# Exps over three PSUM banks and odd score tiles in the attention part of a ViT tower on one Trainium2 core

## The reference

```python
h = tok_embed(x)                                   # 16 x 1024 x 64
# attention on layernorm(h), 8 heads of 8 dimensions
scores = einsum('bihd,bjhd->bhij', q, k) / sqrt(8) + col_bias[None, :, None, :]
attn = softmax(scores, axis=-1)
h = h + einsum('bhij,bjhd->bihd', attn, v).reshape(B, N, D) @ Wo + bo
# experts on layernorm(h): 8 experts of 64 hidden units, the best 2 of a softmax router
h = h + tokens + sum_e combine[:, e] * (gelu(tokens @ w1[e] + b1[e]) @ w2[e] + b2[e])
```

## Time and profile before

| | us |
|---|---|
| median of three runs | 1386.28 |
| the profiled execution | 1381.28 |
| its span, first to last instruction | 1379.5 |
| TensorE matmuls busy | 1237.4 (90%) |
| VectorE busy | 833.8 (60%) |
| ScalarE busy | 1050.4 (76%) |
| mean granted TensorE clock | 0.985 of full speed |

### The profile page before, as it was taken

How to read it: one execution, slowest core, us unless ns; L and a number is a source line. 1 busy time by engine, 2 the same in 40 slices (tenths; PEclk the granted TensorE clock), 3 DMA queues, 4 the chain that set the end, 5 groups by cost and what they waited for, 6 DMA issues and landing times. The chain is left out here.

```text
span 1379.5 us, 29786 instructions
## 1 busy us (share of the span) xinstructions
PE 1237.4 (90%) x9442; PEld 368.5 (27%) x9443; DVE 833.8 (60%) x2165; ACT 1050.4 (76%) x1173; POOL 116.6 (8%) x113
## 2 busy tenths in 40 slices
PE   2179999998989898999999999999999988999998
PEld 1021222322222222222222222222222222333332
DVE  8734566575756575756565757565666256655555
ACT  0069998988889898989999999898989963333333
POOL 4300000000001000000000000000000000000000
PEclk9999999999999999999999999999999988999999
DMA  1222132322222222212131313131223011222221
GB/s 43 55 52 72 41 79 66 70 56 62 66 57 70 45 71 45 71 45 71 45 82 34 82 34 82 34 82 42 76 50 73 10 57 39 57 73 62 62 74 42
DMA packets 63101, 80.31 MB, mean 58 GB/s; under 512 B 26960, under 2 KB 27984, under 8 KB 63000
## 3 DMA queue, kind: packets, MB, share of 16 engines
q1 hardware_dynamic: 60828, 78.76, 22.7%
q10 hardware_dynamic: 1916, 0.55, 0.2%
q0 software_dynamic: 256, 0.01, 0.0%
HBM read 41.90 MB, written 37.27 MB: 57 GB/s over the span
## 5 line engine op out<-in xcount | busy, mean ns | idle before, releaser
L1025 ACT ACTIVATE probs<-psum 128x1024 f32<-128x1024 f32 x1024 | 956.6, 1080 | 91.1 <-PE psum L1154 86.9
L1170 PE MATMUL psum<-probs,VA 128*32 128x512 f32 x4096 | 553.5, 612 | 21.7 <-ACT probs L1025 16.1
L1154 PE MATMUL psum<-QA,KA 54*128 54x512 bf16 x2048 | 351.4, 389 | 36.7 <-ACTq L1044 9.0
L1154 PEld LDWEIGHTS psum<-QA,KA 54*128 54x128 bf16 x2048 | 81.6, 93 | 541.1 <-ACT probs L1025 511.1
L1308 ACT ACTIVATE act_h<-psum,b 128x512 f32<-128x512 f32 x128 | 87.8, 687 | 143.8 <-PE psum L1411 137.7
L1359 DVE TENSOR_TENSOR gated<-act_h,psum 128x512 f32<-128x512 f32 x128 | 87.8, 687 | 90.3 <-ACT act_h L1308 90.1
L1071 DVE STREAM_TRANSPOSE oT<-psum 128x512 f32<-128x512 f32 x64 | 45.9, 717 | 154.0 <-issue 85.5
L1170 PEld LDWEIGHTS psum<-probs,VA 128*32 128x32 f32 x4096 | 83.9, 108 | 150.0 <-issue 91.4
L1411 PE MATMUL psum<-m_x,w_parts 128*128 128x512 bf16 x384 | 108.3, 392 | 1.1 <-DMA m_cT<-cT_d 1.1
L1383 PE MATMUL psum<-gated,w 128*64 128x512 f32 x256 | 69.9, 624 | 0.0
L1025 ACT ACT_TABLE_LOAD x1 | 1.3, 1283 | 76.2 <-issue 76.2
(11 more groups left out here) (187 smaller groups left out, 1015.6 us busy)
## 6 DMA issues: line engine op xcount, KB each, us to landing
QA<-q_parts_d SPq DMA_DIRECT2D x64, 192.0 KB
KA<-k_parts_d SPq DMA_DIRECT2D x64, 192.0 KB
q_parts_d<-qk_parts SPq DMA_DIRECT2D x32, 192.0 KB, 2.5
k_parts_d<-qk_parts SPq DMA_DIRECT2D x32, 192.0 KB, 2.7
xT<-in_xT SPq DMA_DIRECT2D x16, 256.0 KB, 3.5
q_parts_d<-qk_parts SPq DMA_DIRECT2D x32, 128.0 KB, 2.6
k_parts_d<-qk_parts SPq DMA_DIRECT2D x32, 128.0 KB, 2.6
x_d<-x_stacks SPq DMA_DIRECT2D x16, 256.0 KB, 2.1
```

Of the source, the lines that this page charges most:

```text
L1025: nc.scalar.activation(probs[:, k % PROB_BUFS, :], score_buf(buf_of(k)), ACT.Exp).then_inc(exped, 1)
L1154: last = pe.matmul(score_buf(buf_of(k))[:, (g % 2) * BANK:(g % 2 + 1) * BANK], KA[rows_of(h, SCORE_ROWS), h // 2, jt * P:(jt + 1) * P], QA ...
L1170: last = pe.matmul(o_acc[32 * g:32 * g + 32, :], VA[:, jt, h, :], probs[:, k % PROB_BUFS, (g % 2) * BANK:(g % 2 + 1) * BANK], start=(jt == ...
```

## The change

A score *tile* is now three banks, or two for the last tile of each group of 32 scores: 10 x 3 + 2 = 32, so 11 tiles a group and 44 exps an image. PSUM holds two score buffers of three banks, `probs` four buffers of three banks. A tile no longer coincides with half a quad: `TILE_OF` gives the tile of each score, and on TensorE the small steps of a slot and the values of a quad are issued in the turn of the tile that completes the quad (values two tiles later). The thresholds of semaphores follow. The fallback keeps buffers of two banks.

```diff
-SCORE_BUFS = 3
-PROB_BUFS = 8
+WIDE = 3
+GROUP_TILES = [WIDE] * 10 + [2]
+TILES = GROUPS * len(GROUP_TILES)
+FIRST = ...  # first score of each tile
+TILE_OF = [t_ for t_ in range(TILES) for _ in range(FIRST[t_], FIRST[t_ + 1])]
+SCORE_BUFS = 2
+PROB_BUFS = 4
...
-                    nc.scalar.activation(probs[:, k % PROB_BUFS, :], score_buf(buf_of(k)),
+                    n = FIRST[t + 1] - FIRST[t]
+                    nc.scalar.activation(probs[:, t % PROB_BUFS, 0:n * BANK], score_buf(t)[:, 0:n * BANK],
                                          ACT.Exp).then_inc(exped, 1)
...
-                def scores(b, q):
-                    for g in range(4):
-                        k = 2 * q + g // 2
-                        if g % 2 == 0:
-                            if last_use(k) >= 0 or later(b):
-                                pe.wait_ge(exped, BLOCKS * b + last_use(k) + 1)
-                        h, ih, jt = head_of(q, g)
-                        last = pe.matmul(score_buf(buf_of(k))[:, (g % 2) * BANK:(g % 2 + 1) * BANK],
+                def scores(b, t):
+                    if t >= SCORE_BUFS or later(b):
+                        pe.wait_ge(exped, TILES * b + t - SCORE_BUFS + 1)
+                    for n, i in enumerate(range(FIRST[t], FIRST[t + 1])):
+                        h, ih, jt = head_of(i // 4, i % 4)
+                        last = pe.matmul(score_buf(t)[:, n * BANK:(n + 1) * BANK],
                                          KA[rows_of(h, SCORE_ROWS), h // 2, jt * P:(jt + 1) * P],
                                          QA[rows_of(h, SCORE_ROWS), h // 2, ih * BANK:(ih + 1) * BANK],
                                          start=True, stop=True)
-                        if g % 2:
-                            last.then_inc(scored, 1)
+                    last.then_inc(scored, 1)
...
-                    for q in range(QUADS):
-                        ...
-                        scores(b, q)
-                        for step in steps_of(q, not last, not first):
-                            ...
-                        if q >= LAG:
-                            values(b, q - LAG)
-                        elif not first:
-                            values(b - 1, QUADS + q - LAG)
+                    for t in range(TILES):
+                        ...
+                        scores(b, t)
+                        for slot in range(QUADS):
+                            if TILE_OF[4 * slot + 3] != t:
+                                continue
+                            for step in steps_of(slot, not last, not first):
+                                ...
+                        for q in range(QUADS):
+                            if TILE_OF[4 * q + 3] == t - LAG:
+                                values(b, q)
+                            elif TILE_OF[4 * q + 3] == t - LAG + TILES and not first:
+                                values(b - 1, q)
```

More of the change, by code:

```diff
@@ L40 @@
 QUADS = 2 * 2 * NCH
-BLOCKS = 2 * QUADS
 GROUPS = 4
+QUARTER = QUADS // GROUPS
+WIDE = 3
+GROUP_TILES = [WIDE] * 10 + [2]
+TILES = GROUPS * len(GROUP_TILES)
+FIRST = [0]
+for g_ in range(GROUPS):
+    for n_ in GROUP_TILES:
+        FIRST.append(FIRST[-1] + n_)
+TILE_OF = [t_ for t_ in range(TILES) for _ in range(FIRST[t_], FIRST[t_ + 1])]
 LAG = 2
-SCORE_BUFS = 3
-PROB_BUFS = 8
+SCORE_BUFS = 2
+PROB_BUFS = 4
 EVAC_SLOTS = {8 * g + 7 + LAG: g for g in range(3)}
@@ L52 @@
 POST = ["out_proj", "post_t0", "post_t1", "router", "combine_t"]
-ROUTER_EXP_BLOCK = 52
-BUF_TURN = 38
+ROUTER_EXP_TILE = 36
 PAIRS = NX // 2
@@ L198, in attention, with score_buf, fb_buf @@
         oT_norm = sb("oT_norm", [P, 2, BANK // 32, 32], F32)
[L200 to L209, removed]
+        def score_buf(t):
+            return psum[:, WIDE * BANK * (t % SCORE_BUFS):WIDE * BANK * (t % SCORE_BUFS + 1)]
+        def fb_buf(u):
+            return psum[:, 2 * BANK * (u % 2):2 * BANK * (u % 2 + 1)]
         o_acc = psum[:, 6 * BANK:7 * BANK]
@@ L1048, in body @@
                     flag = act.value_load(flags[0:1, ds(b, 1)], min_val=0, max_val=1)
[L1049 to L1053, removed]
+                    for t in range(TILES):
+                        if t % (TILES // 2) == 0:
+                            fallback(b, t // (TILES // 2), flag)
+                        exp_tile(b, t)
+                        if t == ROUTER_EXP_TILE and not first:
                             router_exp(aux_base(b) + aux_order(not last, True).index("router") + 1)
@@ L1184, in fallback @@
                             for n in range(2):
-                                last = pe.matmul(score_buf(u % 2)[:, n * BANK:(n + 1) * BANK],
+                                last = pe.matmul(fb_buf(u)[:, n * BANK:(n + 1) * BANK],
                                                  QA[rows_of(h, SHIFT_ROW), h // 2, c * P:(c + 1) * P],
@@ L1201, in body @@
                     order = aux_order(not last, not first)
[L1202 to L1213 removed]
+                    for t in range(TILES):
+                        if t % (TILES // 2) == 0:
+                            hg = t // (TILES // 2)
+                            pe.wait_ge(aug_loaded[hg], 16 * AUG_DMAS * (b + 1))
+                            fallback(b, hg, flag)
+                        scores(b, t)
[3 more added lines that the diff above has]
+                            for step in steps_of(slot, not last, not first):
+                                i = order.index(step)
+                                aux_step(step, b + 1 if step in PREP else b - 1, aux_base(b) + i + 1, aux_base(b) + i)
+                        for q in range(QUADS):
[3 more added lines that the diff above has]
+                                values(b - 1, q)
                 all_batches(pe, body)
[L1216 to L1217 removed]
+                for q in range(QUADS):
+                    if TILE_OF[4 * q + 3] >= TILES - LAG:
+                        values(NB - 1, q)
         inner.close()
```

27 lines of the change are left out of this document (14 added, 13 removed).

## The result

Four runs of the changed kernel took 1443.47 to 1457.21 us, the median 1451.34 us, against 1386.3: slower, ratio 1.0475 (95% interval 1.0409 to 1.0540). Forecast were 1435 us and 1403 to 1462. The profiled execution took 1443.5 us (62.2 us more than before's), so it is the fastest of the four, and the others had a lower mean clock (0.979 to 0.981 against 0.984). Two executions of the kernel before are left out of the comparisons: one of 2225.99 us beside the changed kernel's four, and one of 1436.38 us at a mean clock of 0.849 beside e5, e7, e8 and e9.

What follows compares the result with a forecast made beforehand. The prediction took ScalarE and TensorE as nearly equal bounds. TensorE's 62.3 us plus 5.5, 0.1 and 2.3 of waiting, less 0.9 and 0.3, gave 69.0 an image: 1435 us in all, range 1403 to 1462.

Steps and rivals of the forecast that it cites:

- Two bounds almost on top of each other: In a middle image of the kernel before, ScalarE needs 58.2 us plus stalls and TensorE 62.3, of 65.8.
- Wider exps, -1.0 us: On ScalarE, fewer and wider exps take 57.2 us an image in place of 58.2.
- Odd tiles, +5.5 us of TensorE: A tile of three scores costs what four did, 0.535 us, adding 5.5 us an image on TensorE.
- Rival C: Between small steps ScalarE keeps the pace and its saving of 1.0 to 1.2 us an image arrives: 1369 us, chance 0.07.
- Rival A: Left-over scores pair with the next tile's first at three places a group: no change, 1386 us, chance 0.06.
- Mutual waiting, 12 x 0.2: With two score buffers, TensorE waits 0.2 us for an exp three times a group: 2.3 us an image.
- Rival D: The two-buffer hand-over is worse, say 0.1 us of stall at every tile: +4.8 us an image, 1463 us, chance 0.11.
- Small steps: Steps between scores and values show nearly whole on ScalarE: one stall of about 1.3 us behind the projections, 0.8 at the transposes.
- VectorE: TensorE's waits for VectorE: 0.9 us before the post transposes and 0.3 before a group's first values go; image start +0.1.
- Sum: A middle image takes 69.0 us: 66.7 of TensorE and 2.3 of mutual waiting, +3.2 us.
- The clock: Stretches of lower TensorE clock behind the embedding add about 0.3 us an image, the same as before the change.
- Rival B: A TensorE with less idle time loses the low-clock stretches, and half the mutual waiting is absent: 1413 us, chance 0.14.

Runs made afterwards that it cites:

- e5: The kernel before with values three quads behind their scores in place of two (LAG = 3): 1621.5 us, ratio 1.172.
- e7: The changed kernel without the fallback's branches on VectorE, TensorE and ScalarE: 1408.9 us, ratio 1.018 to the kernel before.
- e8: The kernel before without the fallback's branches on VectorE, TensorE and ScalarE: 1352.8 us, ratio 0.977.
- e9: The changed kernel with six more, useless score matmuls ahead of each image's first values, where TensorE idles: 1442.8 us, ratio 1.044 to the kernel before.
- e3: The changed kernel with exps of at most two banks from the second image on, a third of their columns left out: 1436.0 us, ratio 1.038.
- e12: The changed kernel without the fallback's branches, third score matmul of each tile narrowed to 64 columns from the second image on: 1351.8 us, ratio 0.978.
- e11: The changed kernel without the fallback's branches, each three-score tile given a fourth matmul repeating its second score: 1413.8 us, ratio 1.022 to the kernel before.
- e1: The kernel before with two score buffers of two banks in place of three: 1443.2 us, ratio 1.043.
- e13: The kernel before with the scores of quad 3 issued directly behind the embedding, ahead of the first values: 1378.4 us, ratio 0.996.
- e4: The changed kernel with score tiles of four and two banks by turns, so every tile has whole pairs: 1602.6 us, ratio 1.159 to the kernel before.
- e10: The kernel before with LAG = 3 and VectorE's evacuations of slots 2 and 18 moved ahead of those slots' small steps: 1456.0 us, ratio 1.052.

## Why the prediction was right, point by point

- *Two bounds almost on top of each other.* Right. e3 shows that ScalarE no longer bounds; in e8 58 us of the 63.74 of an image are exps, which shows how little it was away from bounding before.
- *Wider exps, -1.0 us.* Right in the duration (1.34 from start to start). Of the 1.0 us, 0.3 an image is what e12 has over e8.
- *Odd tiles, +5.5 us of TensorE.* Right: 0.53 for three, as for four. e11 and e12 show it. Rival C (a tile of three at the time of two) fell. Rival A's pairing happens (0.75 for six at 736.87), but in one place an image and not in twelve, and the tile after the pair then waits 0.41 us for its exp (739.09); the time did not follow A. The prediction had expected it in two to four places, yet counted none in its sum.
- *Mutual waiting, 12 x 0.2.* Right: exps 1, 2, 5, 6, 12, 16, 23, 24, 27, 34, 38 and 39 of an image (counted from 0) start 0.14 to 0.19 late, with and without branches, 2.1 us in all. They are not three in every group, as forecast, but four, two, three and three. With the small steps' stalls there are 21 places, 11.1 us, in a full-clock image (709 to 778 us); forecast were 19 and 11.5. Rival D, a stall at every tile and 70.6 us an image, fell. e1 shows that the number of buffers matters by itself (+3.3 us), and e12 that two buffers of three banks are enough as soon as TensorE has room. So the cost is the two together; how much each has of it no run separates.
- *Small steps.* The stall of 1.3 behind the projections is there (1.22 of idle at 733.72), 0.75 at the transposes.
- *VectorE.* The 0.9 in front of the post transposes went. The 0.3 for an evacuation did not go: it is 0.66 (765.92) and gives ScalarE a stall of 0.8. At the turn of the loop TensorE waits 0.89, not 0.46; before, the values of one more quad had lain in it. The wait at the image's start was forecast at 1.4 to 1.5. It comes in two sizes, with the time that VectorE stands in "issue" ahead of its evacuation: 0.6 to 0.7 us in five of the middle images (5.8 to 5.9 us of issue) and 1.3 to 1.5 in eight (6.5 to 6.7, as in most images before). Why VectorE takes one or the other stays open.
- *Sum.* 69.0 us for a middle image; 68.6 to 68.7 at full clock, and 69.3 in the ninth, where the wait at the image's start is as long as forecast.
- *The clock: the term that was mis-sized.* I took 0.3 us an image, as before. Seven of the fifteen images have a low stretch and take 70.4 to 72.1 us, 2.2 more than the others. Not all of the 2.2 is the clock: in these images VectorE is late as well. Its evacuation in a full-clock image and in one with a low stretch, then TensorE in the latter:

```profile
714.25 0.72 DVE L1074 STREAM_TRANSPOSE oT<-psum 128x512 f32<-128x512 f32 x1 [5.93 <-issue]
360.86 0.72 DVE L1074 STREAM_TRANSPOSE oT<-psum 128x512 f32<-128x512 f32 x1 [6.55 <-issue]
```

```profile
358.38 1.95 PE L554 MATMUL psum<-w_tok,xT 64*128 64x64 f32 x16
361.68 1.93 PE L1171 MATMUL psum<-probs,VA 128*32 128x512 f32 x8 [1.35 <-ACT probs L1028]
363.54 1.03 PE L1155 MATMUL psum<-QA,KA 54*128 54x512 bf16 x3
364.50 1.32 PE L1171 MATMUL psum<-probs,VA 128*32 128x512 f32 x8
365.76 0.60 PE L1155 MATMUL psum<-QA,KA 54*128 54x512 bf16 x3
```

  The profile puts TensorE's wait of 1.35 us down to an exp; the evacuation ends at 361.58, 0.1 us before the values start, and they need it too. Values of 1.86 for 1.00, scores of 0.96 for 0.53. The ninth image has the same idle time (1.30 us) and no low stretch, and takes 69.3 us: so 0.6 of the 2.2 is the longer idle time, which the forecast had in its sum, and 1.6 the low stretch. Before, an image with a low stretch took 0.8 more than one without at about the same idle time (five of the six; the sixth took nothing more). The stretches are hardly more (seven, one of them of 6.8 us, against six), but each costs twice as much. That TensorE has no room left that would hide it fits this, and no run tests it. The prediction's reading of the stretch was off as well: its window holds only part of it, and TensorE is at half of full speed for the whole of 3.4 us, from 675.0 on:

```profile
675.00:678.40 3.40, 3.40 (x16) 0.35 (x15) 3.04 (x14) 1.10 (x2) 0.00 (x0) 0.50 0.18 44
```

  The low stretches of the changed kernel come to 12 us in the profiled execution (seven times 1.6, and 1 for the long one), those of the kernel before to 4. These 8 are most of the 10 us by which the attention part (+60) lies above the forecast's +50. The 3.4 us ahead of the first exp and the lower clock of the other executions are most of what is left of the 16 us between forecast and median. Rival B expected the reverse, a busier TensorE that loses the stretches; the idle time behind the embedding stayed, and so did they. Where e7 and e9 take the idle time away they go (all but the first image's in e7, all in e9's profiled execution).

What stays open: which images get a low stretch. In the changed kernel idle time of 1.3 to 1.5 us behind the embedding goes with it in seven images of eight, in the kernel before in five of eleven with 1.2 to 1.5 us. Nor are such idle times needed: one image before has a stretch behind 0.38 us of idle, and in e13, whose embedding is followed at once by scores, they stand behind 0.8 to 1.4 us a little later, one of the seven behind none over 0.3.

## What to carry to other kernels

Where matmuls run in pairs on two halves of the array, a buffer should hold whole pairs: an odd count costs a full slot each time that the next buffer must be waited for, and a spare matmul of the other half tests that in one run. Before a change takes slack from the second-busiest engine, add up its work per round, with the waits it already has: here 62 of 66 us were taken, and a saving of 1 us met a cost of 5.5. When instructions move, look at what stands ahead of them on every engine (e5), and whether a hidden wait becomes an idle TensorE (e4).

## What the hardware showed that was not expected

- 40 more matmuls an image (e11) cost 0.26 us an image: a matmul on the other half of the rows beside a running one takes under 0.01 us.
- TensorE's clock was half of full speed (1.2 of 2.4 GHz) in stretches of 3.4 to 10.2 us of the attention part. Nearly all began during an idle time of TensorE or within 2 us of its end (one in e13 did not), and short ones go with it: seven of fifteen images of the changed kernel behind 1.3 to 1.5 us, one before behind 0.38, stretches of 10.2 us in e4 behind 3.4 us and behind 0.84 and 1.58. With the values at once behind the embedding there were none in the middle images of e7, e8 and e12; those of e10 stood behind idle times of 1.4 to 2.2 us elsewhere in the image.
- VectorE stands 5.7 to 6.8 us in "issue" at the image's start, where its program has a loop turn and one branch that is not entered, and 2.7 us there in e7, without the branch. Without the fallback's branches on three engines the kernel before is 2.3% faster (e8), more than any change of order gave.
